# Attention and expert kernel: products with V in pairs of key blocks, three runs of small products a step, the next row chain a step sooner, another lead-in

## The reference

```
q = layernorm(x) heads 16 x 32, scaled by 32**-0.5
k, v = the two halves of ctx (16, 512, 1024)
logits = q @ k.T + b + MASK * (key >= length of the batch)
x = x + tanh(g0) * softmax(logits) @ v
h = layernorm(x)
logits8 = cosine of h with 8 centroids + h @ w_route.T
gates = softmax over the two largest of the 8
x = x + tanh(g1) * sum_e gates_e * (gelu(h @ w1_e + b1_e) @ w2_e + b2_e)
```

## Time and profile before

| | us |
|---|---|
| median of 3 runs | 1891.76 (1890.41 to 1893.55) |
| the profiled execution | 1897.25 |
| its span, first to last instruction | 1895.5 |
| mean granted TensorE clock | 0.978 |
| busy: TensorE | 1733.6 (91%) |
| busy: VectorE | 1382.8 (73%) |
| busy: ScalarE | 1185.8 (63%) |
| busy: POOL | 1269.8 (67%) |

### The profile page before, as it was taken

One profiled execution on the slowest core, in us unless ns is written; L12 is line 12 of the kernel. 1 busy time (PEld: TensorE's weight loads), 2 busy tenths in 40 slices (PEclk: granted clock), 3 DMA queues, 4 the chain that ended last, 5 costly groups with the idle time before them and its releaser, 6 DMA issues. The chain is left out here.

```text
span 1895.5 us, 32938 instructions
## 1 busy us (share of the span) xinstructions
PE 1733.6 (91%) x9696; PEld 1041.0 (55%) x9697; DVE 1382.8 (73%) x2997; ACT 1185.8 (63%) x2048; POOL 1269.8 (67%) x1491
## 2 busy tenths in 40 slices
PE   1799999999999999999999999995499999999997
PEld 1344555555555555555555555543377777777775
DVE  6767887878878878788788787743666676666675
ACT  3357677677676776776767767662355555555554
POOL 2348577567585766675857666661378888888887
PEclk9999999999999999999999999996599999999999
DMA  5979899899898998998989978834278887978784
GB/s 111 182 123 187 160 172 184 130 201 163 149 200 156 171 183 135 197 165 147 201 154 171 185 126 173 141 104 139 79 136 154 151 150 156 162 132 155 147 150 70
DMA packets 173067, 291.45 MB, mean 154 GB/s; under 512 B 37982, under 2 KB 42078, under 8 KB 172944
## 3 DMA queue, kind: packets, MB, share of 16 engines
q1 hardware_dynamic: 140016, 222.26, 60.8%
q0 software_dynamic: 32928, 67.68, 20.3%
HBM read 127.09 MB, written 71.63 MB: 105 GB/s over the span
## 5 line engine op out<-in xcount | busy, mean ns | idle before, releaser
L1038 DVE TENSOR_REDUCE bank<-bank 128x1 f32<-128x512 f32 x1024 | 696.5, 691 | 257.6 <-PE bank L808 249.6
L676 ACT ACTIVATE prob<-bank 128x512 f32<-128x512 f32 x1024 | 592.9, 597 | 363.3 <-PE bank L796 361.8
L621 POOL TENSOR_TENSOR prob<-prob 128x512 f32<-128x512 f32 x256 | 320.8, 1290 | 330.0 <-PE bank L742 330.0
L796 PE MATMUL bank<-stB,stA 100*128 100x512 f32 x1024 | 477.8, 467 | 22.0 <-ACT prob L676 13.6
L808 PE MATMUL bank<-stA,stB 98*128 98x512 f32 x1024 | 424.0, 416 | 31.5 <-DMA stA<-regrouped_then_w 16.8
L796 PEld LDWEIGHTS bank<-stB,stA 100*128 100x128 f32 x1024 | 193.7, 190 | 256.0 <-ACT prob L676 176.5
L625 POOL TENSOR_TENSOR prob<-prob 128x512 f32<-128x512 f32 x256 | 320.4, 1287 | 0.0
L742 PE MATMUL bank<-prob,vin 128*32 128x512 f32 x2048 | 273.6, 606 | 0.7 <-ACT prob L676 0.7
L1304 POOL DMA_INDIRECT out_dram<-yout,scatter_ids x144 | 241.5, 1677 | 44.0 <-issue 41.3
L808 PEld LDWEIGHTS bank<-stA,stB 98*128 98x128 f32 x1024 | 198.3, 194 | 78.8 <-DVE bank L1038 37.6
L1274 POOL DMA_INDIRECT rows_in<-xn_rows,gather_ids x152 | 166.2, 1094 | 85.2 <-DVE rows_in L1489 44.2
(11 more groups left out here) (190 smaller groups left out, 2221.6 us busy)
## 6 DMA issues: line engine op xcount, KB each, us to landing
stB<-regrouped_then_w SPq DMA_DIRECT2D x192, 256.0 KB, 5.8
stA<-regrouped_then_w SPq DMA_DIRECT2D x192, 256.0 KB, 6.8
x_k_then_w<-in_x_dram SPq DMA_DIRECT2D x16, 1024.0 KB, 8.0
x_k_then_w<-in_ctx_dram SPq DMA_DIRECT2D x16, 1024.0 KB, 11.7
vin<-in_ctx_dram SPq DMA_DIRECT2D x16, 1024.0 KB, 9.2
xres<-in_x_dram SPq DMA_DIRECT2D x16, 1024.0 KB, 6.8
out_dram<-xres SPq DMA_DIRECT2D x16, 1024.0 KB, 7.5
xn_rows<-xn SPq DMA_DIRECT2D x64, 256.0 KB, 5.4
```

The costliest lines, as they stand in the source:

```text
L621: pool.tensor_tensor(first[:, j, :], first[:, j, :], more[:, j, :], ALU.add).then_inc(s_acc, 1)
L676: act.activation(prob_of(st, 0, u)[:, j, :], psS[j % 2][:, :], ACT.Exp).then_inc(s_exp, 1)
L796: pe.matmul(psS[j % 2][:, :], stA[0:100, g, j, kt * P:(kt + 1) * P], stB[0:100, g, j, :], start=True, stop=True).then_inc(s_qk, 1)
L1038: dve.tensor_reduce(mx[:, s // 4, s % 4:s % 4 + 1], psM[s % 2][:, :], AX.X, ALU.max).then_inc(s_mx, 1)
```

## The change

V's blocks go in pairs: blocks 0 and 1 in slot 9 of their own step, blocks 2 and 3 in slot 2 of the next, the sums alone in slot 5. All four blocks of `prob` rotate. MT, DT, OT, XT, LG move one slot back, and with them what ScalarE and VectorE do with them; `attT` is copied in slot 3, `sumT` in 6. The routing scores are read in slots 0 and 1 of the step after. `query_scale` moves to the last step of the batch before, `normalise_q` to slots 1, 5, 9, 13. In the lead-in ScalarE fills both stacks, issues the placing of k rows and the first rows of maxima itself, MT of step -1 comes ahead of its slots, and `set_routes` runs two steps later.

```diff
-TURNS = [("TQ", 3), ("SM", -1), ("TK", 3), ("MT", 1), ("DT", -1), ("OT", -1), ("XT", -5), ("LG", -5)]
+TURNS = [("TQ", 3), ("TK", 3), ("SM", -1), ("MT", 1), ("DT", -1), ("OT", -1), ("XT", -5), ("LG", -5)]
-        for name, off in TURNS:
+        for name, off in sorted(TURNS, key=lambda turn: turn[0] != "MT") if n == -1 else TURNS:
...
-                return prob[:, u if u >= 2 else (st.l + off + u) % 2, :, :]
+                return prob[:, (st.l + off + u) % NT, :, :]
...
@@ SP @@
+                        if st.l < 1:
+                            sp.wait_ge(s_ones, 2 * g + 2)
...
+                        if st.l >= 0:
+                            sp.wait_ge(s_full, st.count(2, 3, 2))
+                            place_rows(stA, 1, g, 0, turnedH)
...
-                    if st.on(1):
+                    if st.on(1) and st.l >= 0:
...
@@ POOL @@
-                pool.memset(stB[96:P, :, :, :].bitcast(F32), 1.0).then_inc(s_ones, 1)
...
-                    elif st.g() == 0 and st.on(4):
+                    if st.g() == 3 and st.on(5) and st.l > -5:
                         query_scale(pool, st)
...
@@ ScalarE @@
+                def place_k(st):
+                    g = st.g(3)
+                    for part, src in ((0, turnedH), (2, turnedH), (1, turnedL)):
...
+                        act.dma_start(stA[DH * part:DH * (part + 1), g, :, :].bitcast(F32),
+                                      src[:, 1, :].bitcast(F32)).then_inc(s_stk[1], 16)
...
+                    if st.l == -1:
+                        take_maxima(st)
...
+                            act.dma_start(stB[98 + t:99 + t, 0, :, :].bitcast(F32), ...
...
-                                act.wait_ge(s_pv, st.count(PV, -1, (2, 1, 3, NT)[u]))
-                                if u in (0, 2):
+                                act.wait_ge(s_pv, st.count(PV, -1, (2, 3, NT, NT)[u]))
+                                if u <= 1:
                                     act.wait_ge(s_acc, st.count(ADDS, -1, ADDS if u else HG))
...
-                        if st.g() == 0 and s in (7, 9, 12, 14) and st.on(4):
+                        if st.g() == 0 and s in (1, 5, 9, 13) and st.on(4):
...
+                    for stack in (stA, stB):
+                        act.activation(stack[96:P, g, :, :]...
@@ TensorE @@
-                        if j == 1 and u > 0 and st.on(0):
-                            values(st, 0, u - 1)
-                        if s == 1 and st.on(-1):
-                            values(st, -1, NT - 1)
                         if s == 2 and st.on(-1):
+                            values(st, -1, 2)
+                            values(st, -1, 3)
+                        if s == 9 and st.on(0):
+                            values(st, 0, 0)
+                            values(st, 0, 1)
+                        if s == 5 and st.on(-1):
                             sums(st, -1)
...
@@ VectorE @@
-                    if st.l == -4:
-                        query_scale(dve, st)
+                        query_scale(dve, Step(None, -5, G))
+                    if st.l == -2:
                         set_routes()
...
-                        if s == 10 and st.on(-1):
+                        if s == 11 and st.on(-1):
...
-                        if s == 11 and st.on(-1):
+                        if s == 12 and st.on(-1):
...
-                        if s in (12, 13) and st.on(-1):
-                            column_stats(st, 2 * (s - 12))
-                        if s == 14 and st.g() == 0 and st.on(-4):
+                        if s in (13, 14) and st.on(-1):
+                            column_stats(st, 2 * (s - 13))
+                        if s == 15 and st.g() == 0 and st.on(-4):
                             row_stats(st)
```

More of the change, by code:

```diff
@@ L770, in turn_rows, with turn_maxima @@
                     last.then_inc(done, 1)
+                def turn_maxima(st):
+                    pe.wait_ge(s_nm, st.count(2, 1, 2))
+                    bank, done = put_turn(pe, st, "MT")
+                    for i in range(NT):
+                        last = pe.transpose(bank[0:2 * HG, i * P:(i + 1) * P],
+                                            nm[:, i, :, :].rearrange("p t h -> p (t h)").bitcast(F32), ident[:, :])
+                    last.then_inc(done, 1)
                 def turn_routes():
@@ L817, in step @@
                             turn_rows(st, s // 3)
-                        if s == 5 and st.on(1):
-                            pe.wait_ge(s_nm, st.count(2, 1, 2))
-                            bank, done = put_turn(pe, st, "MT")
-                            for i in range(NT):
-                                last = pe.transpose(bank[0:2 * HG, i * P:(i + 1) * P],
-                                                    nm[:, i, :, :].rearrange("p t h -> p (t h)").bitcast(F32), ident[:, :])
-                            last.then_inc(done, 1)
-                        if s in (7, 9) and st.on(-1):
-                            name, src = ("DT", sumT) if s == 7 else ("OT", attT)
-                            if s == 7:
+                        if s == 6 and st.on(1) and st.l >= 0:
+                            turn_maxima(st)
+                        if s in (8, 10) and st.on(-1):
+                            name, src = ("DT", sumT) if s == 8 else ("OT", attT)
+                            if s == 8:
                                 b, before = turn_of(st, "SM")
@@ L841, in step @@
                             last.then_inc(done, 1)
-                        if s == 14 and st.on(-5):
+                        if s == 15 and st.on(-5):
                             b, before = turn_of(st, "XT")
```

75 lines of the change are left out of this document (41 added, 34 removed).

## The result

The changed kernel takes 1975.38 us (median of 6 runs, 1974.18 to 1979.06), the kernel before on the same chip 1891.67 (6 runs, 1888.59 to 1894.03): a ratio of 1.0454, 95% interval 1.0443 to 1.0464, 84 us slower. The forecast was 1908, in a range up to 1927. The sign was right, the size was not. The profiled span is 1972.4 us with a mean granted clock of 0.935; before it was 1895.5 at 0.978.

A forecast was written before the change was run, and what follows sets the result against it. The prediction took TensorE as the bound, with VectorE a second limit that decides slots 10 to 2 after the change. Steady steps + 18, lead-in - 5, tail + 3 gave + 16 on 1891.8: 1908 us, range 1888 to 1927.

The forecast's parts named there:

- The walk: Steady steps: VectorE's list limits slots 10 to 2, TensorE the rest; batch 77.0 against 75.8, plus 18 us over 15 batches.
- The pair of blocks: TensorE's paired V runs: 1.86 us a pair, taken from the column sums, against 2.00 for two single runs.
- rival (b): V runs on TensorE: a pair costs two singles, 2.00, so 1926 us; chance 0.13.
- Rival (a): Steady steps: TensorE alone decides and VectorE's walk is hidden, 1847 us; chance 0.14, whole or half.
- Rival (d): Lead-in falls by 13 us and VectorE's stretch is a little shorter: no change, about 1892 us; chance 0.08.
- rival (e): TensorE's clock falls with the added waits, 10 us a step over 60 steps, about 2500 us; chance 0.01.
- Lead-in: Before the steady steps: ScalarE's fill and earlier issuing make it 5 us sooner; bounds 3 later to 13 sooner.
- Tail: Last step: V's first block comes in slot 9 instead of 5, some 2.5 later; plus 3 us.
- POOL's adds: They start in slot 9 instead of 5 and end before exp 4 of the next step, covered by 2.5 us.
- Rival (c): POOL's adds decide: 1 us late beyond the slack is 60 us, 1968 us; chance 0.04.
- Normalising sooner: q row chain a step earlier: cost zero; removes about 1 us of exp waits, worth nothing where VectorE decides.
- Sum: Whole kernel: + 18 - 5 + 3 = + 16 on 1891.8, so 1908 us; chance 0.60.

The follow-up runs named there:

- experiment 4: The changed kernel plus eight zero products of 128 columns a step on TensorE ahead of the waiting maxima products: 1931.24 us, ratio 1.0224.
- 6: The changed kernel with LayerNorm pieces spread, V blocks 0 and 1 paired in slot 10, 2 and 3 paired in slot 1: 1836.41 us, ratio 0.9731.
- 9: The kernel with LayerNorm spread, one V pair and two single V blocks, its column statistics computed four times: 1991.89 us, ratio 1.0544.
- experiment 8: The kernel before the change with its column statistics computed twice on VectorE, nothing else moved: 1929.71 us, ratio 1.0211.
- Experiment 7: The kernel with LayerNorm spread, one V pair and two single V blocks, its lead-in bulk loads held behind the k rows: 1825.76 us, ratio 0.9653.
- experiment 11: The changed kernel with query_scale and the four q normalisings back in the first step of a batch: 2001.87 us, ratio 1.0579.
- kernel 10: The kernel with LayerNorm spread and all V blocks paired, its column statistics computed three times: 1985.27 us (1935.86 to 1995.02).

## Why the prediction was right or wrong

**The walk was right.** The forecast took 11.3 us from the maxima product of slot 2 to that of slot 10, and 7.7 from there on. The trace has 804.99 to 816.30, 11.31, and to 824.32, 8.02 in a step with the row statistics, for which 7.68 + 0.5 had been given. Steps that no fall touches take 18.98 (12, 16, 32, 36, 48, 56 among the first of a batch, 11 and 31 among the last), forecast 19.0; a second one 19.86 (step 17), forecast 19.6. The pair of blocks is 1.85, forecast 1.86, so rival (b), a pair at the price of two singles, is out. Rival (a), TensorE alone, is out: its idle time before L841 is where the forecast put it. Rival (d) is out with the lead-in, 1.4 sooner and not 13.

**The step that failed is rival (e) and the chance that it got.** The prediction named the mechanism, in the right place, and gave it 1 in 100, on the ground that the granted clock "is 1.00 through today's waits". That row says only that today's waits are short and apart: a mean of 0.18 and 0.11 us in slots 12 and 13 of a step, 0.06 in slot 0. The walk in the same text had put 7.68 us on a stretch for which TensorE wants 6.5, so more than 1 us of waits in nine neighbouring slots, and the row of before couldn't speak for that. The second half of the error is the price. It was worked out as all or nothing, all of TensorE's own 11.3 us of every step at the lower level, 2500 us. The clock came back each time in slot 2, in 33 of 37 falls while the pair of blocks ran, where TensorE works without a wait; a fall lasts 4.2 us in the mean (157 / 37). The measured price is the time above the walk per time at the lower level: 54 / 157 = 0.34 after the change, 0.34 to 0.52 over the seven kernels of the table with six falls or more. With products 0.43 apart instead of 0.23, a TensorE that never waits would lose some 0.47 us for each us at the lower level. That the changed kernel loses less fits with VectorE catching up while the products are slow, so that waits fall away; this wasn't tested by itself. With 37 falls that is 54 us, and with it the sum would have been 1908 + 54 = 1962. Most of the 13 that are still missing are in the tail (10) and the lead-in (4), below.

The granted clock of 0.50 behind the 0.86 us wait shows the swing, and experiment 4 its cause. The Trainium skill has it ("TensorE: Matmul & The Clock Gate", the section on a second failure mode): short idles between groups of products, repeated often, make the clock swing between its two levels. The trace agrees with it: 37 falls in 60 steps, none in the kernel before.

**What the falls go with.** The changed kernel's falls go with waits that stand together (slots 14, 15 and 2) and not with the pairs (experiments 4, 6, 9) nor with the idle total alone (experiment 8). How the length of the waits and their distance act on the clock separately wasn't tried.

**Lead-in: minus 1.4, forecast minus 5.** The parts came as said: the cast takes 0.40, normalising starts at 17.21 (forecast 17.3), the first maxima product at 39.31, 2.9 sooner. Even the first logits product is 3.5 sooner (73.5, it was 77.0). Then the bulk loads, now ahead of the last k rows, let the maxima product of step 0 wait 7.38 us, and step 0 took 25.2 instead of 20.4; step 1, with 17.8 instead of 20.5, gave 2.7 back. This was in the bound ("3 later, bulk ahead of the k rows") and not in the value taken. Experiment 7 shows that the loads held up that product, and that putting them behind the rows doesn't save it: the DMA engines are full in the mean up to 110 us, and the wait came up elsewhere.

**Tail: plus 12.8, forecast plus 3; that the whole stretch after step 62 came out at plus 3.6 is luck.** From the start of step 62 to the first rank product it is 93.8 us, it was 81.0, and the unchanged expert phase happened to be 9.2 shorter. The forecast had the last sums 2.5 later; they start 45.3 us after step 62 does, where it was 34.6, 10.7 later. In the kernel with filler it is 41.1, 6.5 later. The walk left out that the steps 62 and 63 are longer themselves (the first takes 17.84 instead of 15.96), and the clock: from the start of step 62 to the first product of the expert table its mean is 0.71, it was 0.83.

**POOL's adds: covered, as said**; done at 825.24, the exp at 827.14, a slack of 1.9 where 2.5 was given. Rival (c), POOL's adds decide, is out.

**Normalising sooner: no cost forecast, and the gain inside the sum.** That held: TensorE has next to no wait for exps left at that place. But the prediction called the slack worth nothing where VectorE decides, and without it the first step of a batch waits 1.3 us for an exp; experiment 11 gives 26 us for the edit.

**Sum.** Forecast + 16; the terms as measured in the spans: - 1.4 + 20 (walk, 15 x 1.3, since a batch before is 75.7) + 55 (clock) + 12.8 (tail) - 9.2 (expert phase, scatter) = + 77. With the clock up in steps 2 to 61 the change would have been about 1919 (experiment 4), inside the range.

## What to carry to other kernels

Where a change puts a row of waits of a few tenths of a microsecond on a TensorE that is 97% busy, walk the waits and then ask what the clock does with them; the row of before, with shorter waits, doesn't answer that. Price a falling clock by the stretch behind the waits, here 0.3 to 0.5 us for each at the lower level, not by the whole kernel. Measure each term between two events of its own: a part that nobody touched can hide it. And give long runs of products with no reader to wait for to the stretch where VectorE has most to do: splitting one pair and spreading the LayerNorm's pieces turned 1975 into 1828 us.

## What the runs showed of the hardware

- In the changed kernel the granted clock falls, for 4.2 us in the mean, on a TensorE that is busy 97% of the time (870.47 of 900 us): 37 times in 60 steps, 44 and 48 times with longer waits. Eight extra products of zero a step took 36 of 37 falls away and 44 us off.
- It isn't the same in each execution of a kernel: kernel 10 took 1936 us once and 1983 to 1995 three times.
- VectorE's cast of 128x512 integers takes 0.40 us when POOL isn't filling memory beside it; beside a fill of 6.92 us it took 6.95.
- The granted clock dropped in the lead-in of kernel 7, where a product waited 5.67 us for a transfer: it is 0.50 from 95.7 to 105.9 us, and the product behind the wait, at 99.13, is listed at 0.79.
